# The last unit's last normalisation in a four-layer graph kernel, applied and stored in two halves of 256 tokens

## What is computed

```python
x = _layernorm(x + _L0_gnn_ref(x, ..., adj))        # attention with one head
x = _layernorm(x + _L1_gnn_ref(x, adj, weight, bias))
x = _layernorm(x + _L2_gnn_ref(x, ..., adj))        # attention with eight heads
x = _layernorm(x + _L3_gnn_ref(x, adj, adj, ...))   # three steps of a gated recurrence

def _layernorm(x, axis=-1, eps=1e-05):
    m = jnp.mean(x, axis=axis, keepdims=True)
    v = jnp.var(x, axis=axis, keepdims=True)
    return (x - m) / jnp.sqrt(v + eps)
```

## Time and profile before

| What | us |
|---|---|
| median of 3 executions | 1404.07 |
| lowest and highest of them | 1403.95, 1404.28 |
| profiled execution, its own time | 1404.12 |
| its span in the profile | 1402.0 |

### The profile page before, as it was taken

One profiled execution on the slowest core, in us unless ns is written; L12 is line 12 of the kernel. 1 busy time (PEld: TensorE's weight loads), 2 busy tenths in 40 slices (PEclk: granted clock), 3 DMA queues, 4 the chain that ended last, 5 costly groups with the idle time before them and its releaser, 6 DMA issues.

```text
span 1402.0 us, 26908 instructions
## 1 busy us (share of the span) xinstructions
PE 1343.0 (96%) x10423; PEld 1139.1 (81%) x10423; DVE 1059.1 (76%) x2367; ACT 790.7 (56%) x1450; POOL 143.3 (10%) x196
## 2 busy tenths in 40 slices
PE   6888999999999999999999999999999999999896
PEld 5767888888888888888888888888888787888784
DVE  5797778778787878778777777877778786868455
ACT  3546556556655565656566565655666555564453
POOL 5211100110010110001011000001101010100000
PEclk9999999999999999999999999999999999999998
DMA  5010010100000001000000000010000000000000
GB/s 175 1 27 21 1 24 31 23 30 15 7 30 22 30 15 37 0 22 30 22 30 15 22 15 22 30 22 30 15 7 30 23 31 9 31 8 32 16 0 30
DMA packets 54653, 34.52 MB, mean 25 GB/s; under 512 B 34896, under 2 KB 51536, under 8 KB 54608
## 3 DMA queue, kind: packets, MB, share of 16 engines
q1 hardware_dynamic: 52800, 29.43, 7.1%
q0 software_dynamic: 1248, 3.94, 0.9%
q10 hardware_dynamic: 560, 0.52, 0.1%
HBM read 12.92 MB, written 8.39 MB: 15 GB/s over the span
## 4 chain that ended last, share of the span: by engine, by line
PE 68%; DVE 16%; ACT 7%; issue 4%; POOL 3%; DMA 1%; SPq 0%; ACTq 0%; POOLq 0%; DVEq 0%
PE banks L121 16%; PE banks L123 15%; PE banks L122 15%; PE banks L587 8%; PE banks L582 3%; PE banks L746 2%; ACT y L273 2%; PE banks L650 2%; PE banks L731 2%; PE banks L720 2%; DVE l_stats L245 2%; PE banks L848 1%; DVE l_r L2415 1%; DVE l_r L2408 1%; DVE l_sum L2255 1%
## 5 line engine op out<-in xcount | busy, mean ns | idle before, releaser
L1515 ACT ACTIVATE l_r<-banks,bias_r 128x512 f32<-128x512 f32 x90 | 61.7, 686 | 179.2 <-PE banks L123 179.1
L259 POOL TENSOR_TENSOR l_rstd<-l_mv,eps 128x4 f32<-128x4 f32 x48 | 25.6, 534 | 889.6 <-DVE l_mv L253 889.6
L1532 ACT ACTIVATE banks<-banks,bias_h 128x512 f32<-128x512 f32 x96 | 63.2, 659 | 64.8 <-PE banks L123 64.8
L2154 DVE TENSOR_TENSOR l_rh_lo<-l_r,l_rh_hi 128x512 fp32r<-128x512 f32 x90 | 61.7, 688 | 28.2 <-ACT l_rh_hi L1381 28.0
L2415 DVE SCALAR_TENSOR_TENSOR l_r<-banks,l_r 128x512 f32<-128x512 f32 x90 | 61.7, 687 | 26.3 <-ACT banks L1526 24.6
L1526 ACT ACTIVATE banks<-banks,bias_z 128x512 f32<-128x512 f32 x96 | 63.3, 660 | 26.3 <-PE banks L123 26.2
L273 ACT ACTIVATE y<-l_sum,l_offset,l_rstd 128x256 f32<-128x256 f32 x128 | 70.6, 592 | 12.1 <-DVE l_offset L267 11.1
L587 PE MATMUL banks<-adj_t,y 128*128 128x128 f32 x544 | 71.1, 280 | 2.8 <-ACT y L273 2.7
L121 PE MATMUL banks<-l_rh_hi,u_hi 128*128 128x512 f32 x180 | 73.6, 409 | 0.0
L2397 DVE SCALAR_TENSOR_TENSOR l_r<-l_r,l_h 128x512 f32<-128x512 f32 x60 | 40.8, 682 | 41.2 <-ACT l_r L1515 41.2
L587 PEld LDWEIGHTS banks<-adj_t,y 128*128 128x128 f32 x544 | 66.4, 195 | 6.6 <-ACT y L273 3.4
(11 more groups left out here) (296 smaller groups left out, 4364.1 us busy)
## 6 DMA issues: line engine op xcount, KB each, us to landing
x_tok<-in_x_dram SPq DMA_DIRECT2D x15, 512.0 KB, 3.6
l_res<-y SPq DMA_DIRECT2D x15, 512.0 KB, 3.0
out_dram<-l_res SPq DMA_DIRECT2D x15, 512.0 KB, 3.0
l_vpair<-l_vstage SPq DMA_DIRECT2D x32, 128.0 KB, 3.2
w_raw<-in_L_gnn_w_w_dram POOLq DMA_DIRECT2D x3, 512.0 KB, 7.6
qkv_raw<-in_L_gnn_w_qkv_dram POOLq DMA_DIRECT2D x1, 768.0 KB, 4.5
l_res<-in_x_dram SPq DMA_DIRECT2D x1, 512.0 KB, 5.2
u_raw<-in_L_gnn_u_w_dram POOLq DMA_DIRECT2D x2, 256.0 KB, 7.6
```

Of the source, the lines that this page charges most:

```text
L1515: nc.scalar.activation(own(u).r[:, m, :], rz(u)[:, m, :], ACT.Tanh, scale=0.5, bias=w.biases["r"][:, m:m + 1]).then_inc(s.r_ready.of(u), 1)
L1532: nc.scalar.activation(hv(u)[:, m, :], hv(u)[:, m, :], ACT.Tanh, bias=w.biases["h"][:, m:m + 1]).then_inc(s.hv_ready.of(u), 1)
L2154: return nc.vector.tensor_tensor(parts[1][:, k, :], bank, parts[0][:, k, :].bitcast(F32), ALU.subtract)
```

## The change

Unit 15's last normalisation is cut into two halves of two tiles (256 tokens). A class `HalfNorm` has the parts of `Norm` for one half, working on two columns of the small tensors. In each half, ScalarE applies the first tile and VectorE the second (`apply_on_vector`, a `tensor_scalar` that multiplies by the root and adds the offset), and each half is stored by its own DMA of 256 KB. VectorE takes residual, statistics and aggregation of half 0, then those of half 1, then offset and application of half 0, then those of half 1. The other units stay as they are. One new semaphore (`y3_odd`) tells SyncE that VectorE has done its tile; two semaphores used only at the start, `l0_chain` and `const_chain`, become one (`start_chain`), counted on from 4.

```diff
+class HalfNorm:
...
+    def tiles(self, half):
+        return slice(2 * half, 2 * half + 2)
+
+    def statistics(self, dve, u, half, z):
+        for t in (2 * half, 2 * half + 1):
+            ins = self.p.nc.vector.bn_stats(self.norm.stats[:, t, :], z[:, t, :])
+        ins.then_inc(self.norm.stats_done.sem, 1)
+
+    def aggregate(self, dve, u, half):
+        dve.wait_ge(*self.norm.stats_done.at(u, half + 1))
+        self.p.nc.vector.memset(self.norm.carrier[:, :], 0.0)
+        for t in (2 * half, 2 * half + 1):
+            ins = self.p.nc.vector.bn_aggr(self.norm.mv[:, t, :], self.norm.stats[:, t, :])
+        ins.then_inc(self.norm.var_ready.sem, 1)
+
+    def root(self, pool, u, half):
+        n, two = self.norm, self.tiles(half)
+        pool.wait_ge(*n.var_ready.at(u, half + 1))
+        self.p.nc.gpsimd.tensor_tensor(n.rstd[:, two], n.mv[:, two, 1], self.p.eps[:, two],
+                                       ALU.add).then_inc(n.eps_added.sem, 1)
+        pool.wait_ge(*n.eps_added.at(u, half + 1))
+        self.p.nc.gpsimd.tensor_tensor(n.rstd[:, two], n.rstd[:, two], self.p.minus_half[:, two],
+                                       ALU.pow).then_inc(n.rstd_ready.sem, 1)
+
+    def take_offset(self, dve, u, half):
+        n, two = self.norm, self.tiles(half)
+        dve.wait_ge(*n.rstd_ready.at(u, half + 1))
+        self.p.nc.vector.scalar_tensor_tensor(n.offset[:, two], n.mv[:, two, 0], -1.0, n.rstd[:, two],
+                                              ALU.mult, ALU.mult).then_inc(n.offset_ready.sem, 1)
+
+    def apply_on_scalar(self, act, u, half, z):
+        n, t = self.norm, 2 * half
+        act.wait_ge(*n.offset_ready.at(u, half + 1))
+        return self.p.nc.scalar.activation(z[:, t, :], z[:, t, :], ACT.Identity, scale=n.rstd[:, t:t + 1],
+                                           bias=n.offset[:, t:t + 1])
+
+    def apply_on_vector(self, dve, u, half, z):
+        n, t = self.norm, 2 * half + 1
+        dve.wait_ge(*n.offset_ready.at(u, half + 1))
+        return self.p.nc.vector.tensor_scalar(z[:, t, :], z[:, t, :], n.rstd[:, t:t + 1], n.offset[:, t:t + 1],
+                                              op0=ALU.mult, op1=ALU.add)
...
+        def store_last(half):
+            two = pair_of(half)
+            sp.wait_ge(*s.y3.at(UNITS - 1, half + 1))
+            sp.wait_ge(s.y3_odd, half + 1)
+            sp.dma_start(dst[UNITS - 1][:, two, :], own(UNITS - 1).res[:, two, :]).then_inc(s.stored.sem, 16)
...
             l3_store(14)
-            l3_store(15)
+            store_last(0)
+            store_last(1)
...
         run(sp, fill, body, drain)
-        sp.wait_ge(*s.stored.at(UNITS - 1, 16))
+        sp.wait_ge(*s.stored.at(UNITS - 1, 32))
...
             l3_root(14)
-            l3_root(15)
+            last_norm.root(pool, 15, 0)
+            last_norm.root(pool, 15, 1)
...
             for n in range(4):
                 l3_apply(14, n)
-            for n in range(4):
-                l3_apply(15, n)
+            for n in range(2):
+                apply_last(n)
...
+        def statistics_of_last(half):
+            dve.wait_ge(*s.l3_z.at(UNITS - 1, half + 1))
+            dve.wait_ge(*s.y3.at(UNITS - 2, 1))
+            last_norm.statistics(dve, UNITS - 1, half, own(UNITS - 1).res)
...
             for n in range(2):
                 l3_residual(15, n)
-            l3_statistics(15)
-            l3_variance(15)
-            l3_offset(15)
+                statistics_of_last(n)
+                last_norm.aggregate(dve, 15, n)
+            for n in range(2):
+                last_norm.take_offset(dve, 15, n)
+                apply_last(n)
```

More of the change, by code:

```diff
@@ L126, with __init__ @@
 class Links:
-    def __init__(self, eng, sem):
-        self.eng, self.sem, self.n = eng, sem, 0
+    def __init__(self, eng, sem, n):
+        self.eng, self.sem, self.n = eng, sem, n
     def link(self, ins):
@@ L168, in constants @@
     return adj_blk, hits, count, zeroed, made, loaded
+SUMS_OF_A = 4
 GATES = ("u3", "w4s", "w5s", "diff", "u5")
@@ L191, in __init__ @@
         self.loaded = [p.sem(f"l{n}_w_loaded") for n in range(4)]
-        names = ("l0_chain", "adj_turned", "const_chain", "l0_hi", "l0_ready", "l1_hi", "l1_ready", "qkv_hi", "qkv_ready", "proj_hi", "proj_ready", "summed",
+        names = ("start_chain", "adj_turned", "l0_hi", "l0_ready", "l1_hi", "l1_ready", "qkv_hi", "qkv_ready", "proj_hi", "proj_ready", "summed",
                  "natural", "turned", "gate_hi", "gate_lo", "bias_summed", "bias_ready")
@@ L274, in apply, with __init__ @@
                                            bias=self.offset[:, t:t + 1])
+class HalfNorm:
+    def __init__(self, norm):
+        self.norm, self.p = norm, norm.p
+    def tiles(self, half):
[33 more added lines that the diff above has]
+                                              op0=ALU.mult, op1=ALU.add)
 class Own:
@@ L362, in __init__ @@
         self.l3_z, self.y3 = one("l3_z", 2), one("y3", 1)
+        self.y3_odd = p.sem("y3_odd")
 def fused(p, block, w, b, s, norms, src, dst, started):
@@ L375, in fused @@
     l0, l1, l2i, l2o, l3 = norms
+    last_norm = HalfNorm(l3)
     ws = w.sems
@@ L1359, in high_l0 @@
         def high_l0():
-            act.wait_ge(ws["l0_chain"], 4)
+            act.wait_ge(ws["start_chain"], SUMS_OF_A)
             nc.scalar.activation(w.l0[0][:, :, :], w.l0_raw[:, :, :], ACT.Copy).then_inc(ws["l0_hi"], 1)
@@ L1554, in l3_apply, with apply_last @@
                 ins.then_inc(s.y3.sem, 1)
+        def apply_last(half):
+            last_norm.apply_on_scalar(act, UNITS - 1, half, own(UNITS - 1).res).then_inc(s.y3.sem, 1)
         def body(i):
@@ L2084, in sum_a @@
             else:
-                dve.wait_ge(ws["l0_chain"], n)
+                dve.wait_ge(ws["start_chain"], n)
             if n % 2 == 0:
@@ L2090, in sum_a @@
                 ins = nc.vector.tensor_reduce(w.l0_raw[:, :, DIM + n // 2:DIM + n // 2 + 1], w.wa[:, :, :], AX.X, ALU.add)
-            ins.then_inc(ws["l0_chain"], 1)
+            ins.then_inc(ws["start_chain"], 1)
         def split_low(parts, whole):
@@ L2132, in make_constants @@
         def make_constants():
-            links = Links(dve, ws["const_chain"])
+            links = Links(dve, ws["start_chain"], SUMS_OF_A)
             dve.wait_ge(adj_loaded, 64)
@@ L2444, in l3_statistics, with apply_last @@
             dve.wait_ge(*s.l3_z.at(u, 2))
-            if is_last(u):
-                dve.wait_ge(*s.y3.at(u - 1, 1))
             l3.statistics(dve, u, own(u).res)
+        def statistics_of_last(half):
+            dve.wait_ge(*s.l3_z.at(UNITS - 1, half + 1))
+            dve.wait_ge(*s.y3.at(UNITS - 2, 1))
+            last_norm.statistics(dve, UNITS - 1, half, own(UNITS - 1).res)
+        def apply_last(half):
+            last_norm.apply_on_vector(dve, UNITS - 1, half, own(UNITS - 1).res).then_inc(s.y3_odd, 1)
         l3_variance = within(lambda u: l3.aggregate(dve, u))
```

## The result

The changed kernel takes 1400.85 us, the median of 13 executions (1399.13 to 1402.95); the kernel before, run beside it, 1404.28 (1402.51 to 1405.67). The ratio is 0.9977 with a 95% interval of 0.9969 to 0.9984: faster, by 3.2 us (2.2 to 4.4).

The account below looks back on a forecast made before the run. TensorE bounds the kernel as a whole, but unit 15's normalisation at the end is a serial chain without it. Terms +0.26 - 0.40 - 1.47 + 0.03 - 0.75 = -2.33 gave 1401.7 us, range 1401.2 to 1402.7.

Parts of the forecast that it names:

- term 1: VectorE up to the second aggregation: broken pipelining and two more waits on itself cost +0.26 us (bounds 0.15 to 0.45).
- term 2: GpSimd's root of half 1: power on two columns takes 0.61 in place of 1.01 us, -0.40 (to 0).
- term 3: Last applications on ScalarE: one of 0.60 us in place of four of 2.07, -1.47.
- term 4: SyncE before the last store: waiting for a second semaphore costs +0.03 us (0 to 0.05).
- term 5: Last store: half the bytes at the same rate save 0.75 of 2.9 us (bounds -0.50 and -0.90).
- Rival A: GpSimd's root gets no cheaper and VectorE's application delays its addition up to 0.30: 1402.1, with both 1402.4 us; chance 0.36.
- Rival C: Second store moves nothing until the first has landed, landing 2.15 us later: 1403.6 us; chance 0.03.
- Rival B: Second of two close stores finds its way prepared, saving half a microsecond more: 1401.2 us, over 0.2% faster; chance 0.08.
- Rival D: Longer VectorE and GpSimd lists put a code fetch into the tail: 1404.6 us, or 1407.5 with two; chance 0.03.

Follow-up runs that it names:

- e10: Changed kernel with pieces of three tiles and one, last tile's application shared by columns, VectorE taking both residuals first: 1401.89 us, ratio 0.9984.
- e7: Kernel before with merged start semaphores, plus seven small memsets in VectorE's list: 1403.69 us, ratio 0.9999.
- e2: Kernel before with only the changed kernel's semaphores (the two start chains merged, y3_odd unused): 1403.33 us, ratio 0.9992.
- e6: Kernel before with merged start semaphores, plus two small memsets in GpSimd's list: 1403.64 us, ratio 1.0.
- e3: Changed kernel with one 512 KB store at the end in place of two of 256 KB: 1402.64 us, ratio 0.9986.

## Why the prediction was right in its sum and wrong in its range

| step | predicted | measured |
|---|---|---|
| term 1, VectorE up to the second aggregation | +0.26 | +0.33 |
| term 2, root on two columns | -0.40 (power 0.61) | -0.33 (power 0.69 or 0.70, 1.01 before) |
| term 3, one application in place of four | -1.47 | -1.47 |
| term 4, second wait of SyncE | +0.03 | 0.00 |
| term 5, half the store | -0.75 | -0.8 (5.13 to 5.24 us from issue to end of span, now 4.37 to 4.43; in the first pair of profiles -0.87) |
| first residual to end of span, first pair | -2.33 | -2.34 (12.11 to 9.77) |
| outside the span | 0 (left out of the sum) | -0.37 |

**The terms.** None of them is off by more than 0.12. That their sum is right within 0.01 is luck: terms 1 and 2 fell short by 0.07 each, terms 4 and 5 came out better by 0.03 and 0.12. Term 1: the statistics of half 0 start 0.12 behind the first residual, not 0.05, since the wait for unit 14's application takes longer to be seen; the other steps have the lengths given. Term 2: with e10 there are now powers of one, two, three and four columns, 0.55, 0.70, 0.85 and 1.01: 0.155 for each column on top of 0.39. The row that I leaned on, an addition of 0.20, was the wrong one for the fixed part; a power has twice that. Term 5: the 256 KB store landed in 2.2 us, 0.7 less than the 512 KB store. The estimate from the Trainium skill (DMA: Bandwidth & Descriptors, section on the anatomy of one DMA) was 2.6 for it, and 3.2 against a measured 2.9 for 512 KB; the measurement decides. That section is headed with the path of DMAs that GpSimd issues, and these stores are issued by SyncE. Term 3 and its cover were right: VectorE's application takes 0.41, inside the bounds of 0.24 and 0.48, and is done before ScalarE's.

**Rival A** falls on both counts: the power got cheaper, and the addition stays at 0.19 beside the tensor_scalar. The Trainium skill's rule (GPSIMD Engine Reference, Specifications) can't be said to be refuted by that, since the two operations met at one timing only; for a VectorE operation with two inputs, rows 6 stand. **Rival C** falls: the second store lands in 2.2 us. Its milder form is real, as e10 shows, where one store is issued while another's data are moving. **Rival B** came nearest to the time with its 1401.2, and that outcome, faster by more than 0.2%, had a chance of 0.08; but its cause is wrong: the half store is 0.05 to 0.12 us better than summed, not half a microsecond. **Rival D** did not come: no step of the tail grew by a fetch.

**The step that failed** is the line that takes the sum off "the profiled execution's own 1404.12". Of these 2.12 us lie outside the span, and by taking the -2.33 off the whole I put any change in them at nothing, without a reason and without a term or a bound. They are 0.37 less in the changed kernel, and 0.38 less in e7, which differs from e2 by seven memsets in VectorE's list and a small buffer that e6 has too. Rival D had the right place, a longer list of VectorE, and the wrong sign: I looked for a cost that it could bring into the tail. It also had the wrong count, since "seven rows" is the number of lines by which the printed order of VectorE's list grows; the operations are four more. The sum with the missing term is -2.7 us, and 1404.07 - 2.7 = 1401.4, which lies inside the range.

**The range** failed by its term for the spread of runs. I took 0.3 us for it from three executions within 0.33 us. A hundred and two executions of the same kernel go from 1401.88 to 1406.31. Medians of a dozen carry about half a microsecond of that, and 1400.85 is such a median; the mean of all 35 is 1401.03. From 1401.4 down to these there are 0.4 to 0.55 us that no term explains. The interval of the difference takes them in, so nothing else is needed, but nothing excludes that 0.3 or 0.4 us of them are real.

## What to carry to other kernels

On a tail where every step waits for the one before, a sum of durations from rows, counted from the last event that the change leaves alone, came within 0.12 us in each term here; compare such stretches between profiles, not times from the start of the span, and not single executions, and ask how far two profiles of the same tail differ (0.26 us here) before reading a tenth. Splitting the last piece pays by what it takes off the last link of each stage (here 1.47 for the applications, 0.8 for the store, 0.3 for the root) and costs the hand-overs (0.33); as e10 shows, go on only as long as the small piece finds the slow engine and the store queue free. Before giving a range for an effect of a few microseconds in 1400, ask how far a dozen executions of one kernel lie apart; and don't take the time outside the span for a constant when an engine's list changes its length.

## What was not expected of the hardware

**The spread goes with the granted clock of the first 100 us.** Two executions of the same changed kernel, the first set's profile (1402.15) and the third's (1400.00); columns: stretch, length, busy time of PE, PEld, DVE, ACT and POOL, granted clock, DMA share, GB/s:

```profile
40.00:60.00 20.00, 14.59 (x77) 13.05 (x78) 17.12 (x44) 8.10 (x16) 1.98 (x6) 0.83 0.00 1
60.00:100.00 40.00, 35.80 (x410) 30.83 (x409) 32.18 (x72) 21.87 (x43) 3.64 (x6) 1.00 0.09 21
```

```profile
40.00:60.00 20.00, 15.10 (x96) 12.65 (x95) 17.11 (x45) 9.78 (x19) 2.72 (x6) 0.99 0.00 1
60.00:100.00 40.00, 35.79 (x413) 30.93 (x412) 33.49 (x75) 21.48 (x43) 2.46 (x4) 1.00 0.09 21
```

Between 40 and 60 us the second has a granted clock of 0.99, that is 2.4 GHz nearly throughout; the first has 0.83, so it spent a third of the stretch at 1.2 GHz. The program is the same, and TensorE is busy for three quarters of the stretch in both. From 100 us on the two are alike (1.00 in both up to 1380). The same pair of SyncE's copies is issued at 103.33 us in the first and at 101.41 in the second, so 1.9 us apart; the first residual of unit 15 starts at 1390.53 and 1388.39, 2.1 us apart. Nearly all of it arises in the first 100 us and is carried to the end.

The other profiles agree. All 13 have 1.00 in the long stretches from 100 to 700 and from 700 to 1380 us. Over the first 100 us the granted clock is 0.97 in one, where the first residual starts at 1388.4 us; 0.95 in four, 1388.6 to 1389.9 us; 0.93 in six, 1389.9 to 1390.6; and 0.91 in two, 1390.8 and 1391.0. Only the edit of the start semaphores lies in that stretch, and the kernel before, which alone is without it, stands in the group of 0.93 with five that have it. Of the kernel before, the 18 executions with a mean granted clock of 0.992 average 1402.57 us, the 17 with 0.988 average 1405.49. What makes the clock differ between executions of one program is not shown.

**The time of an execution has a part outside the profile's span that no instruction list shows.** It is 2.18 us before and 1.81 with the change, steady within 0.13 in each kernel. Seven operations more in VectorE's list took 0.37 off it (e7), the store's size (e3) and two more on GpSimd (e6) nothing.
